# First hats from PSUM, nine sums over thirteen product buffers, and other orders, in a deformable attention followed by a binary convolution

## The chip, the cores and the metric

One core of one Trainium2 chip runs the whole kernel. TensorE (PE) multiplies matrices, VectorE (DVE), ScalarE (ACT) and GpSimd (POOL) work elementwise, SyncE (SP) issues DMAs. The metric is the device time of one execution in microseconds, as the median of several runs. All engines work off their own lists in order; semaphores tie them together.

## The reference

The input x is 4 images of 64 channels and 32 by 32 pixels. Two layers follow each other.

The first is a deformable attention with 8 heads of 8 channels and 4 points for each head:

```
v    = q @ W_value + b_value
off  = q @ W_off + b_off            # an (x, y) offset for each pixel, head and point
attn = softmax over the 4 points of (q @ W_attn + b_attn)
loc  = the pixel's own place + off / 32
out  = sum over points of attn * bilinear(v, loc)
x    = out @ W_out + b_out + q
```

The bilinear sample takes four neighbours of each place, with weights that are products of a hat in y and a hat in x, max(0, 1 - distance).

The second is a 3 by 3 convolution of the signs of x (with a bias ahead) with the signs of its weights times their mean magnitude, a batch norm over all images, the residual, and a PReLU with biases.

## The kernel before

**Layout.** Images are taken in two pairs (g = 0, 1), each with 2 x 64 channels on the 128 partitions. The 1024 pixels are two halves of 512 (yh = 0 the upper, 1 the lower).

**Taps instead of gathers.** Offsets are small, so that every sampled neighbour lies among 16 shifts around a pixel: 4 rows (ZERO, OUTER, MINUS, PLUS) by 4 columns (ZERO, MINUS, PLUS, OUTER). OUTER stands for shifts that only occur in a zone of 12 pixels at the borders, and so it is smaller. A half has 16 taps, the kernel 32 (t = 0 to 31, 0 to 15 the upper half). A tap has 512 columns; with OUTER in one direction 384, in both 288. A case in which an offset is larger than that has a general branch that isn't taken here.

**Steps of one tap.** (1) The hats: ACT computes a distance `Abs(u + shift)` into `tab` (L688) and a hat `Relu(1 - tab)` (L695), where `u` is the position, the offset in PSUM with its bias (L680). (2) DVE multiplies the turned probabilities with a hat in y: `attend(n)`, one for each row of taps (L941). (3) POOL multiplies this with a hat in x into `ap`, `weight(t)` (L864); taps 0 and 1 are DVE's own (L951, `DVE_COLUMNS`). `ap` has `RAP` = 6 buffers. (4) PE spreads the 32 weights of heads and points over the 128 channels, `spread(t)` (L508, from tap 8 on L513), into one of two, later three, PSUM buffers. From tap 8 on the taps go in pairs, and the second tap of each pair (9, 11, ..., 31) is "swapped": it uses the other half of PE and reads values from `vswap`, so both taps of a pair run at the same time. (5) DVE multiplies with the shifted values, `product(t)` (L970), into one of `PR` = 12 buffers `prod`. (6) PE projects the product with W_out and accumulates in PSUM, `project(unit)` (L530).

**Sums.** The projection is linear, so two products of the same output rows can be added first and projected once. `SUM_FROM = {1: 2, ...}` says that product 2 is added into product 1, by an accumulating DMA that POOL issues (L871) behind the weight that `SUMS_BEHIND` names. The sum is one unit, so the six sums leave 26 units of 32. A buffer of `prod` is free for product t + PR when its unit is projected or, for the second summand, when the sum has landed (`product`, L960 to L965).

**Orders.** PE's list is written out by hand: the units in `TAPS_AFTER[t]` are projected behind spread t, the rest (`TAPS_AT_END`) after the last spread, with the first row of the convolution ahead of the very last unit. Between a swapped and an unswapped unit PE waits for the one before. Spread t also waits for product t - 2 (later t - 3), and for its weight. DVE's list is the products in order, with the `attend`s behind those that `ROW_AFTER` names.

**The start.** Logits, offsets (`ps_off`) and values of the upper half come first; the softmax is made in three parts (two quarters of the upper half, then the lower half whole); `turn(yh)` transposes the probabilities into PSUM (L493). ACT's order is: two exponentials, two positions, then distances and hats. Lower values, offsets and logits follow among the first spreads.

## Time and profile before

| | us |
|---|---|
| median of 3 runs | 86.0 (85.94 to 86.25) |
| the profiled execution | 85.9 |
| its span, first to last instruction | 84.1 |
| PE busy | 66.5 |
| DVE busy | 58.7 |
| POOL busy | 47.7 |
| ACT busy | 46.2 |

A row of a timeline has the start, the duration, the engine, the line of the kernel and the operation; x8 says that eight records are merged, and the brackets name the idle time ahead and what ended it. A projection or a spread of one tap is eight matmul records on PE, the weights of one tap one record on POOL, and the products of one tap one record on DVE. No row carries the number of its tap; it follows from the order and the sizes. The chain of waits is followed back from the last instruction, at each step to what released it.

### The profile page before, as it was taken

How to read it: one execution, taken by the hardware profiler on the slowest of the kernel's cores; microseconds unless marked ns; L12 is line 12 of the kernel's file. 1: busy time of each engine (PE TensorE's matmuls, PEld its weight loads, DVE VectorE, ACT ScalarE, POOL GpSimd, SP SyncE). 2: the span in 40 equal slices, each digit the busy share in tenths (PEclk: the TensorE clock that was granted, in tenths of full speed). 3: DMA queues.
4: the chain of work that ended last, by engine and by line, in shares of the span. 5: the costliest groups of instructions: out<-in, count | busy, mean ns of one | idle time of the engine just before them, and what ended most of it. 6: DMA issues, size and time to landing. Idle time of an engine off the chain costs nothing.

```text
span 84.1 us, 1712 instructions
## 1 busy us (share of the span) xinstructions
PE 66.5 (79%) x642; PEld 25.4 (30%) x642; DVE 58.7 (70%) x85; ACT 46.2 (55%) x92; POOL 47.7 (57%) x47
## 2 busy tenths in 40 slices
PE   5999997999799999999999959999799985200000
PEld 4766275223142322132323314222223542200000
DVE  2307978999989999596997889203970067689920
ACT  2401999995599999997000399900000397059500
POOL 7970000879999999999999999950000000009000
PEclk9999999999999999999999999999999999995555
DMA  0917865920599980091006638390000000000195
GB/s 9 295 42 253 250 232 123 224 74 0 97 207 213 213 146 1 0 216 37 0 8 134 119 53 134 64 189 4 0 0 0 8 0 0 0 4 0 24 281 194
DMA packets 3897, 8.09 MB, mean 96 GB/s; under 512 B 560, under 2 KB 1584, under 8 KB 3888
## 3 DMA queue, kind: packets, MB, share of 16 engines
q1 hardware_dynamic: 2320, 4.40, 19.1%
q0 software_dynamic: 1120, 2.88, 19.0%
q10 hardware_dynamic: 448, 0.69, 2.6%
q8 instruction: 5, 0.08, 0.4%
q14 instruction: 4, 0.03, 0.1%
HBM read 2.27 MB, written 1.05 MB: 39 GB/s over the span
## 4 chain that ended last, share of the span: by engine, by line
PE 50%; DVE 19%; POOL 10%; issue 8%; DMA 5%; ACT 2%; DVEq 1%; ACTq 0%; POOLq 0%
PE banks L530 21%; PE banks L513 12%; POOL ap L864 10%; DVE prod L970 6%; DMA win<-w_in_dram 5%; PE banks L562 4%; PE banks L476 3%; PE banks L508 3%; DVE prod L1104 3%; PE banks L459 2%; DVE prod L1115 2%; DVE bns L1075 2%; ACT sg L783 2%; DVE ays L941 1%; PE banks L466 1%
## 5 line engine op out<-in xcount | busy, mean ns | idle before, releaser
L864 POOL TENSOR_TENSOR ap<-ays,hat 128x512 f32<-128x512 f32 (+2 forms) x30 | 36.1, 1592 | 9.7 <-ACT hat L695 9.2
L970 DVE TENSOR_TENSOR prod<-banks,vpad 128x1024 f32<-128x1024 f32 (+2 forms) x20 | 22.1, 1114 | 8.2 <-PE banks L530 5.1
L530 PE MATMUL banks<-prod,wo 64*64 64x512 f32 (+2 forms) x208 | 23.1, 547 | 0.7 <-PE banks L530 0.5
L513 PE MATMUL banks<-ap,cst 32*64 32x512 f32 (+2 forms) x192 | 16.9, 567 | 1.5 <-POOL ap L864 1.0
L888 POOL TENSOR_SCALAR prod<-prod,prm,st 128x512 f32<-128x512 f32 x3 | 2.3, 763 | 19.8 <-ACT st L831 19.8
L970 DVE TENSOR_TENSOR prod<-banks,vswap 128x1024 f32<-128x1024 f32 (+3 forms) x13 | 12.6, 975 | 0.0
L530 PEld LDWEIGHTS banks<-prod,wo 64*64 64x64 f32 x208 | 6.9, 132 | 15.1 <-issue 11.1
L513 PEld LDWEIGHTS banks<-ap,cst 32*64 32x64 f32 x192 | 4.3, 130 | 13.7 <-POOL ap L864 8.1
L688 ACT ACTIVATE tab<-u,cst 128x512 f32<-128x512 f32 x12 | 8.3, 716 | 0.1
L871 POOL DMA_DIRECT2D prod<-prod x6 | 7.3, 1217 | 0.2 <-ACT hat L695 0.2
L695 ACT ACTIVATE hat<-tab 128x512 f32<-128x512 f32 x12 | 7.2, 621 | 0.0
L805 ACT ACTIVATE flag<-banks 1x6 f32<-1x6 f32 x1 | 0.2, 165 | 10.5 <-PE banks L521 10.5
L508 PE MATMUL banks<-ap,cst 64*64 64x384 f32 (+2 forms) x48 | 5.1, 506 | 0.6 <-DVE prod L970 0.6
L941 DVE TENSOR_TENSOR ays<-banks,hat 128x512 f32<-128x512 f32 (+1 forms) x8 | 5.0, 650 | 0.6 <-PE banks L493 0.6
L775 ACT ACTIVATE x1n<-banks,prm 128x512 f32<-128x512 f32 x1 | 0.7, 688 | 8.2 <-PE banks L530 8.2
L562 PE MATMUL banks<-sg,wcb 64*64 64x512 bf16 (+2 forms) x84 | 4.6, 351 | 0.2 <-ACT sg L783 0.2
L724 ACT ACTIVATE ex<-lsub 128x256 f32<-128x256 f32 (+1 forms) x3 | 1.4, 483 | 5.1 <-DVE lsub L903 5.1
L476 PEld LDWEIGHTS banks<-win,xs 128*128 128x128 f32 x32 | 3.9, 191 | 1.1 <-DMA win<-w_in_dram 0.6
L476 PE MATMUL banks<-win,xs 128*128 128x64 f32 x32 | 4.0, 273 | 0.1
L459 PE MATMUL banks<-xs,win 128*64 128x512 f32 x16 | 4.1, 611 | 0.0
L580 PE MATMUL banks<-ones 128*128 128x256 f32 x6 | 2.9, 661 | 1.0 <-POOL ones L851 1.0
L718 ACT ACTIVATE lsub<-lsub,cst 128x384 f32<-128x384 f32 (+1 forms) x6 | 3.5, 580 | 0.2
(84 smaller groups left out, 79.3 us busy)
## 6 DMA issues: line engine op xcount, KB each, us to landing
prod<-prod POOLq DMA_DIRECT2D x4, 512.0 KB, 5.4
vswap<-vpad SPq DMA_DIRECT2D x4, 432.0 KB, 5.5
xs<-x_dram SPq DMA_DIRECT2D x3, 256.0 KB, 4.2
prod<-prod POOLq DMA_DIRECT2D x2, 384.0 KB, 5.4
out_dram<-prod SPq DMA_DIRECT2D x2, 256.0 KB, 3.2
wcf<-w_conv_dram SPq DMA_DIRECT2D x1, 288.0 KB, 4.2
wab<-w_abs_dram SPq DMA_DIRECT2D x1, 288.0 KB, 4.2
xs<-x_dram ACTq DMA_DIRECT2D x1, 256.0 KB, 2.9
```

The lines of the kernel that those rows point to most:

```text
L459: mm = pe.matmul(ps_off[yh][d][g * C:(g + 1) * C, :], wp[:, d, :], chunk(xs, g, yh), start=False, stop=True, skip_group_check=True)
L476: mm = pe.matmul(ps_log[part][:, at:at + C], xs[:, g, q:q + P], wp[:, 2, :], start=False, stop=((n + 1) * P == end and g == G - 1), skip_g ...
L508: mm = pe.matmul(spread_into(t)[rows_out, g, 0:size_of(t)], sel_of(g)[rows_in, rows_out], weights_at(t)[rows_in], start=True, stop=True)
L513: mm = pe.matmul(spread_into(t)[quadrant(i, g, t in SWAPPED)[1], g, 0:size_of(t)], sel_of(g)[rows_in, quadrant(i, g)[1]], weights_at(t)[ro ...
L530: mm = pe.matmul(into, wo[rows_in, rows_in], source, start=False, stop=last, skip_group_check=True)
L562: mm = pe.matmul(ps_y[yh][g][rows_out, first_row * W:last_row * W], wcb[rows_in, ky * K + kx, :], sg[rows_in, g, y0:y0 + last_row - first_ ...
L688: nc.scalar.activation(tab[:, n % 4], u[:, d, yh, :], ACT.Abs, bias=cst[:, c_tap + k:c_tap + k + 1]).then_inc(s_abs, 1)
L695: nc.scalar.activation(hat[:, yh, d, k, :], tab[:, m % 4], ACT.Relu, bias=1.0, scale=-1.0).then_inc(s_hat, 1)
L864: pool.tensor_tensor(into, factor, near, ALU.mult).then_inc(s_ap, 1)
L871: pool.dma_start(prod[:, into % PR, :, 0:size_of(into)], prod[:, more % PR, :, 0:size_of(more)], accum_op=ALU.add).then_inc(s_s2[k % len(s ...
L941: nc.vector.tensor_tensor(ays[:, n % RY, at], ps_att[yh][:, at], hat[:, yh, 1, ky, at], ALU.mult).then_inc(s_ay, 1)
L970: nc.vector.tensor_tensor(as_window(t, prod[:, t % PR, g, 0:n]), as_window(t, spread_into(t)[:, g, 0:n]), v_window(t, g), ALU.mult).then_i ...
```

## The change

What each part does:
- `FROM_PSUM`: the first three distances (y ZERO, x ZERO, x MINUS of the upper half) read the offsets in PSUM directly, with the offset's bias, or that bias plus one (`bias_minus`, a new 128x1 operation). The positions of the upper half are computed behind the first three hats and no longer ahead.
- Tap 1's weight goes from DVE to POOL (`DVE_COLUMNS`, `RA` 3 to 1). The softmax scale of the lower half goes from POOL to DVE.
- PE turns the upper probabilities before it computes the upper values, which go to other banks. Spread 0 comes ahead of the second half of the lower logits. The second turn stands behind spread 4 and no longer behind spread 5.
- DVE stores the upper values behind weight 0; product 0 waits for them. The maximum of the lower logits stands behind product 0. The `attend`s have other places.
- `PR` goes from 12 to 13. Nine sums in place of six, with 23 units in place of 26, and other orders of the units.

```diff
-SUM_FROM = {1: 2, 5: 6, 8: 10, 16: 18, 20: 22, 24: 26}
-SUMS_BEHIND = {6: 1, 9: 5, 15: 8, 23: 16, 26: 20, 29: 24}
-DVE_COLUMNS = [2] + [0] * (ROWS - 1)
+SUM_FROM = {0: 1, 8: 2, 12: 10, 5: 4, 13: 9, 18: 16, 26: 24, 25: 17, 20: 22}
+SUMS_BEHIND = {7: 0, 11: 5, 13: 8, 18: 12, 19: 13, 24: 18, 26: 20, 28: 25, 30: 26}
+DVE_COLUMNS = [1] + [0] * (ROWS - 1)
+FROM_PSUM = [(0, 1, ZERO), (0, 0, ZERO), (0, 0, MINUS)]
...
-        RA, RAP = 3, 6
+        RA, RAP = 1, 6
-        PR = 12
+        PR = 13
-        ps_v = [[bank[0], bank[1]], [bank[5], bank[4]]]
+        ps_v = [[bank[2], bank[3]], [bank[5], bank[4]]]
...
-        TAPS_AFTER = {7: [4], 9: [0, 3], 11: [9, 1], 13: [7], 15: [5, 12], 17: [15], 19: [14, 8], 21: [11], 23: [13],
-                      27: [19, 23, 17], 29: [25, 27, 21, 16], 31: [29]}
-        TAPS_AT_END = [24, 28, 30, 20, 31]
+        TAPS_AFTER = {9: [0, 6, 3], 11: [5, 7], 13: [11], 15: [8], 17: [14], 19: [15], 21: [12], 23: [13], 27: [21, 19, 23],
+                      29: [18, 20, 28], 31: [29, 25, 27]}
+        TAPS_AT_END = [30, 26, 31]
...
-            values(0)
             pe.wait_ge(s_sub, 2)
             logits_bias(2)
+            pe.wait_ge(s_cst, 16)
+            turn(0)
+            values(0)
             pe.wait_ge(s_x[1], 32)
             logits(2, range(NCH // 2))
-            pe.wait_ge(s_cst, 16)
-            turn(0)
-            logits(2, range(NCH // 2, NCH))
-            pe.wait_ge(s_u, 2)
-            base_positions(1, 1)
             for taps in SPREADS:
+                if taps[0] == 1:
+                    logits(2, range(NCH // 2, NCH))
+                    pe.wait_ge(s_vp, G)
                 for t in taps:
                     spread(t)
                 if t == 1:
+                    pe.wait_ge(s_u, 2)
+                    base_positions(1, 1)
                     offsets(1, 1)
...
-                if t == 5:
+                if t == 4:
                     turn(1)
...
             def distances(n):
                 yh, d, k = DISTANCES[n]
+                if (yh, d, k) in FROM_PSUM:
+                    act.wait_ge(s_off, POSITIONS.index((yh, d)) + 1)
+                    if k == MINUS:
+                        act.wait_ge(s_bias, 1)
+                    bias = prm[:, p_off + d:p_off + d + 1] if k == ZERO else bias_minus[:]
+                    nc.scalar.activation(tab[:, n % 4], ps_off[yh][d][:], ACT.Abs, bias=bias).then_inc(s_abs, 1)
+                    return
...
-                pool.wait_ge(s_p, products_done(more, G - 1))
+                pool.wait_ge(s_p, products_done(max(into, more), G - 1))
...
-                if t == 6:
-                    pool.wait_ge(s_rec, 3)
-                    pool.tensor_tensor(grouped(prob[:, 1, :]), grouped(ex[:, 1, :]), spread_points(lrec[:, 1, :]),
-                                       ALU.mult).then_inc(s_prob, 1)
...
-            store_upper_values()
             attend(0)
             weight(0)
-            weight(1)
-            softmax_max(2)
-            ROW_AFTER = [0, 3, 6, 7, 9, 9, 9]
+            store_upper_values()
+            ROW_AFTER = [0, 1, 4, 7, 8, 9, 9]
             for t in range(NT * YH):
                 product(t)
                 if t == 0:
+                    softmax_max(2)
+                if t == 1:
                     softmax_sub(2)
                 if t == 2:
                     softmax_sum(2)
                     softmax_recip(2)
+                    softmax_scale(2)
```

How it moves instructions. ACT, from the first exponentials to the hat PLUS in x (tab is a distance, hat a hat, u a position); before:

```order
L724 ACTIVATE ex<-lsub 128x256 [waits sub_ready] x2
L680 ACTIVATE u<-banks,prm 128x512 [waits offsets_ready,params_in]
L680 ACTIVATE u<-banks,prm 128x512 [waits offsets_ready]
L688 ACTIVATE tab<-u,cst 128x512 [waits positions_ready,const_in]
L688 ACTIVATE tab<-u,cst 128x512 [waits positions_ready]
L695 ACTIVATE hat<-tab 128x512 [waits abs_ready]
L688 ACTIVATE tab<-u,cst 128x512 [waits positions_ready]
L695 ACTIVATE hat<-tab 128x512 [waits abs_ready] x2
L688 ACTIVATE tab<-u,cst 128x512 [waits positions_ready]
L695 ACTIVATE hat<-tab 128x512 [waits abs_ready]
```

and now:

```order
L736 ACTIVATE ex<-lsub 128x256 [waits sub_ready] x2
L694 ACTIVATE tab<-banks,prm 128x512 [waits offsets_ready] x2
L707 ACTIVATE hat<-tab 128x512 [waits abs_ready] x2
L694 ACTIVATE tab<-banks,bias_minus 128x512 [waits shifted_bias_ready,offsets_ready]
L707 ACTIVATE hat<-tab 128x512 [waits abs_ready]
L685 ACTIVATE u<-banks,prm 128x512 [waits offsets_ready] x2
L700 ACTIVATE tab<-u,cst 128x512 [waits positions_ready,const_in]
L707 ACTIVATE hat<-tab 128x512 [waits abs_ready]
```

The two positions moved behind the third hat; up to the fourth hat it is ten operations both times.

POOL, from the weights of taps 16 to 18 on (L864 and L877 are weights, L871 and L884 the issues of sums); before:

```order
L864 TENSOR_TENSOR ap<-ays,hat 128x512 [waits spread_ready,hats_ready,ay_ready] x3
L864 TENSOR_TENSOR ap<-ays,hat 128x384 [waits spread_ready,hats_ready,ay_ready] x4
L864 TENSOR_TENSOR ap<-ays,hat 128x288 [waits spread_ready,hats_ready,ay_ready]
L871 DMA prod<-prod 128x1024 [waits products_ready]
L864 TENSOR_TENSOR ap<-ays,hat 128x512 [waits spread_ready,hats_ready,ay_ready] x3
L871 DMA prod<-prod 128x2x384 [waits products_ready]
L864 TENSOR_TENSOR ap<-ays,hat 128x384 [waits spread_ready,hats_ready,ay_ready]
L864 TENSOR_TENSOR ap<-ays,hat 128x512 [waits spread_ready,hats_ready,ay_ready] x2
L871 DMA prod<-prod 128x1024 [waits products_ready]
```

and now:

```order
L877 TENSOR_TENSOR ap<-ays,hat 128x512 [waits spread_ready,hats_ready,ay_ready] x3
L884 DMA prod<-prod 128x1024 [waits products_ready]
L877 TENSOR_TENSOR ap<-ays,hat 128x384 [waits spread_ready,hats_ready,ay_ready]
L884 DMA prod<-prod 128x1024 [waits products_ready]
L877 TENSOR_TENSOR ap<-ays,hat 128x384 [waits spread_ready,hats_ready,ay_ready] x3
L877 TENSOR_TENSOR ap<-ays,hat 128x288 [waits spread_ready,hats_ready,ay_ready]
L877 TENSOR_TENSOR ap<-ays,hat 128x512 [waits spread_ready,hats_ready,ay_ready]
L884 DMA prod<-prod 128x1024 [waits products_ready]
L877 TENSOR_TENSOR ap<-ays,hat 128x512 [waits spread_ready,hats_ready,ay_ready] x2
L884 DMA prod<-prod 128x2x384 [waits products_ready]
L877 TENSOR_TENSOR ap<-ays,hat 128x384 [waits spread_ready,hats_ready,ay_ready]
L877 TENSOR_TENSOR ap<-ays,hat 128x512 [waits spread_ready,hats_ready,ay_ready]
```

The sums into 12 and 13 stand behind weights 18 and 19, that into 18 behind 24, that into 20 behind 26 as before, and the next row is the sum into 25, behind 28.

PE, behind spread 29 (L530 before and L533 now are projections, two rows for each unit, the other line the spreads); before:

```order
L530 MATMUL banks<-prod,wo 64x512 [waits products_ready]
L530 MATMUL banks<-prod,wo 64x512 x3
L530 MATMUL banks<-prod,wo 64x16x2x12 [waits products_ready]
L530 MATMUL banks<-prod,wo 64x16x2x12 x3
L530 MATMUL banks<-prod,wo 64x384 [waits products_ready]
L530 MATMUL banks<-prod,wo 64x384 x3
L530 MATMUL banks<-prod,wo 64x512 [waits units_projected,sums_ready3]
L530 MATMUL banks<-prod,wo 64x512 x3
L513 MATMUL banks<-ap,cst 64x512 [waits products_ready,gpsimd_tap_weights_ready]
L513 MATMUL banks<-ap,cst 64x512 x3
```

and now:

```order
L533 MATMUL banks<-prod,wo 64x512 [waits units_projected,products_ready]
L533 MATMUL banks<-prod,wo 64x512 x3
L533 MATMUL banks<-prod,wo 64x512 [waits sums_ready3]
L533 MATMUL banks<-prod,wo 64x512 x3
L533 MATMUL banks<-prod,wo 64x16x2x12 [waits products_ready]
L533 MATMUL banks<-prod,wo 64x16x2x12 x3
L533 MATMUL banks<-prod,wo 64x512 [waits units_projected,products_ready]
L533 MATMUL banks<-prod,wo 64x512 x3
L533 MATMUL banks<-prod,wo 64x512 [waits sums_ready2]
L533 MATMUL banks<-prod,wo 64x512 x3
```

Before, four units (25, 27, 21, 16) stand between spread 29 and spread 30, the last of them the sum whose buffer product 28 takes. The second piece is the end of the list now, behind spread 31: units 29, 25, 27, 30, 26.

## Rows read from the trace of the kernel before

**Rows 1.** Chain of waits: start, us, what, where it leaves POOL and at its last projection
```profile
48.47 1.86 POOL ap L864
50.33 0.04 issue
50.37 0.88 PE banks L513 x8
...
66.11 0.73 PE banks L530 x8
```

**Rows 2.** Timeline of PE from spread 24 on
```profile
47.44 1.95 PE L513 MATMUL banks<-ap,cst 32*64 32x512 f32 x24
50.37 0.88 PE L513 MATMUL banks<-ap,cst 32*64 32x384 f32 x8 [0.98 <-POOL ap L864]
51.18 2.22 PE L530 MATMUL banks<-prod,wo 64*64 64x384 f32 x24
53.33 1.11 PE L513 MATMUL banks<-ap,cst 32*64 32x512 f32 x16
54.37 2.38 PE L530 MATMUL banks<-prod,wo 64*64 64x512 f32 x24
...
57.95 1.09 PE L513 MATMUL banks<-ap,cst 32*64 32x512 f32 x8
...
60.49 1.09 PE L530 MATMUL banks<-prod,wo 64*64 64x512 f32 x8 [0.17 <-DVE prod L970]
61.75 3.45 PE L530 MATMUL banks<-prod,wo 64*64 64x512 f32 x32 [0.18 <-PE banks L530]
65.14 0.19 PE L521 MATMUL banks<-over,ones 128*1 128x6 f32 x2
```

**Rows 3.** Timeline of POOL: single weights (L864), issues of sums (L871), the softmax scale
```profile
15.04 1.28 POOL L864 TENSOR_TENSOR ap<-ays,hat 128x512 f32<-128x512 f32 x1 [9.18 <-ACT hat L695]
17.82 1.00 POOL L864 TENSOR_TENSOR ap<-ays,hat 128x384 f32<-128x384 f32 x1 [0.55 <-DVE ays L941]
21.68 1.15 POOL L880 TENSOR_TENSOR prob<-ex,lrec 128x512 f32<-128x512 f32 x1
26.20 1.21 POOL L871 DMA_DIRECT2D prod<-prod  x1 [0.16 <-ACT hat L695]
32.89 1.44 POOL L864 TENSOR_TENSOR ap<-ays,hat 128x384 f32<-128x384 f32 x1
33.83 1.35 POOL L871 DMA_DIRECT2D prod<-prod  x1
...
43.39 0.96 POOL L871 DMA_DIRECT2D prod<-prod  x1
...
46.46 1.65 POOL L864 TENSOR_TENSOR ap<-ays,hat 128x512 f32<-128x512 f32 x1
47.69 1.61 POOL L871 DMA_DIRECT2D prod<-prod  x1
48.47 1.85 POOL L864 TENSOR_TENSOR ap<-ays,hat 128x384 f32<-128x384 f32 x1
...
50.66 2.12 POOL L864 TENSOR_TENSOR ap<-ays,hat 128x512 f32<-128x512 f32 x1
```

**Rows 4.** Timeline of ACT: the first of the ten operations and the last
```profile
8.96 0.69 ACT L680 ACTIVATE u<-banks,prm 128x512 f32<-128x512 f32 x1
...
14.25 0.63 ACT L695 ACTIVATE hat<-tab 128x512 f32<-128x512 f32 x1
```

**Rows 5.** Timeline of DVE: the lower maximum, and products 0, 12 and 28
```profile
14.76 0.68 DVE L897 TENSOR_REDUCE lmax<-banks 128x128 f32<-128x512 f32 x1
15.45 1.23 DVE L970 TENSOR_TENSOR prod<-banks,vpad 128x1024 f32<-128x1024 f32 x1
...
34.54 1.23 DVE L970 TENSOR_TENSOR prod<-banks,vpad 128x1024 f32<-128x1024 f32 x1 [0.87 <-PE banks L513]
...
58.08 1.23 DVE L970 TENSOR_TENSOR prod<-banks,vpad 128x1024 f32<-128x1024 f32 x1 [5.05 <-PE banks L530]
```

**Rows 6.** The line of the six sums' DMAs
```profile
DMA to landing us min/median/max: 4.8/5.4/6.7
```

More of the change, by code:

```diff
@@ L166, in deformable_attention_then_binary_conv @@
         st = sb("st", [P, 17])
+        bias_minus = sb("bias_minus", [P, 1])
         spare = prod[:].rearrange("p r g n -> p (r g n)")
@@ L211, in deformable_attention_then_binary_conv @@
         s_abs = sem("abs_ready")
+        s_bias = sem("shifted_bias_ready")
         s_hat = sem("hats_ready")
@@ L724, in exponentials @@
                 nc.scalar.activation(ex[:, yh, first:end], lsub[:, yh, first:end], ACT.Exp).then_inc(s_exp, 1)
+            act.wait_ge(s_prm, 16)
+            nc.scalar.activation(bias_minus[:], prm[:, p_off:p_off + 1], ACT.Identity, bias=1.0).then_inc(s_bias, 1)
             exponentials(0)
             exponentials(1)
-            act.wait_ge(s_prm, 16)
+            distances(0)
+            distances(1)
+            hats(0)
+            hats(1)
+            distances(2)
+            hats(2)
             positions(0, 1)
@@ L731, in _ @@
             act.wait_ge(s_cst, 16)
-            distances(0)
-            distances(1)
-            hats(0)
-            distances(2)
-            hats(1)
-            hats(2)
             distances(3)
@@ L954, in product @@
                 yh, ky, kx = tap_of(t)
+                if t == 0:
+                    dve.wait_ge(s_vp, G)
                 if yh == 0 and ky == PLUS:
```

## The prediction

> **What bounds the kernel now.** I read the chain of waits first, then PE's timeline, POOL's, and those of ACT and DVE at the places that these two point to. Up to 50.33 us the chain runs over POOL's tap weights, and from there to 66.84 over PE, apart from one product of DVE [rows 1]. So two laws hold in turn. Until spread 27 POOL sets the time: its weight of tap 27 ends at 48.47 + 1.85 = 50.32, and PE's spread 27 starts at 50.37, after 0.98 of idle time [rows 2, 3]. From then on PE has a list to work off, and it ends with the projection of tap 31 at 66.11 + 0.73 = 66.84 [rows 1]. Behind that stand the signs, the rest of the convolution, the batch norm and the output; the change touches none of it. I keep these 84.1 - 66.84 = 17.3 us, and ask when the projection of tap 31 ends now.
>
> **POOL, up to spread 27 (the term that is easy to miss).** POOL's records start ahead of its work (that of the issue at 33.83 starts 0.50 before the weight of 32.89 ends), so I count from end to end. What changes:
> - Start. POOL's weight 2 waits for the hat of column PLUS, the tenth operation of ACT after the two exponentials: from 8.96 to 14.88 [rows 4]. The change reorders these ten and leaves their number: two distances, two hats, a distance and a hat now come ahead of the two positions. The distances read PSUM; a position that reads PSUM today takes 0.69, an operation on SBUF about as much (0.63) [rows 4]. So this hat ends at about 14.9 again, and weight 2 starts at 15.1 where it started at 15.04 [rows 3]: +0.04. POOL's extra weight, tap 1, goes into the 9.18 us that POOL idles here [rows 3]: it needs the sixth of those operations, done at some 12.5, and ends at 13.9. Cost nothing; without that gap 1.3. The small operation that makes the shifted bias stands where ACT waits for the logits, and costs nothing either.
> - The idle 0.55 us ahead of weight 4, for DVE's second row product [rows 3], goes: by the count of DVE below that product is done at 16.6, before weight 3 ends (17.3). -0.55.
> - The softmax scale of the lower half leaves POOL: -1.15 [rows 3]. So does the wait for a hat ahead of sum 5: -0.16 [rows 3].
> - Sums. Each is a DMA that POOL issues between two weights. Its price, from the end of the weight before to the end of the issue: 33.83 + 1.35 - (32.89 + 1.44) = 0.85 for a sum of 512 columns, 47.69 + 1.61 - (46.46 + 1.65) = 1.19 for one of 384 [rows 3]. Ahead of weight 27 there were five (into 1, 5, 8, 16, 20) and now seven (into 0, 5, 8, 12, 13, 18, 20). The two more are of 512 columns: +1.70, and I add 0.1 for the restart behind them.
>
> Sum: 50.32 + 0.04 - 0.55 - 1.15 - 0.16 + 1.80 = 50.3. Weight 27 ends where it ended; what POOL gains is spent on the new sums. Between weights 27 and 29 there was no sum and now stands one (into 25): weight 29 ended at 50.66 + 2.12 = 52.78 [rows 3] and now ends 0.85 later, at 53.6. Between 29 and 31 stands one sum as before, so weight 31 is 0.85 later too, at some 56.7 by the same 3.1 us.
>
> **Is anything else later than POOL at spread 27?** DVE's product 0 started at 15.45 [rows 5]. Now the turn and the hat come earlier, and DVE has the first row product and weight 0 done at 12.6, the two value stores (0.7 each, moved behind them) at 14.0, and product 0 starts when spread 0 ends, about 14.25: -1.2. Between product 0 and 12 DVE now also has the maximum that stood ahead of it (0.68, [rows 5]) and the scale from POOL (some 0.65): +1.3. It was free for product 12 at 34.54 - 0.87 = 33.67 [rows 5], and is so at about 33.8. Nothing is won at the front. PE reached spread 24 at 47.44 [rows 2]; from product 12 to there it has 768 columns of projection less (units 8, 14, 15, 12, 13 behind spread 14, for 5, 12, 15, 14, 8, 11, 13), 1.3 us by the price below. So PE is there at 45.6, or at 46.6 if DVE is an us late, and waits for POOL. Product 24, which spread 27 needs, ends by 48.9 even then. That is the cover of 1.4 to 2 us under which every delay of DVE and ACT ahead of it costs nothing; were it gone, each us would be one of the end.
>
> **PE from spread 27 on.** The price of a run of projections: 1920 columns (24, 28, 30, 20) from 61.75 to 65.14 are 3.39; 1184 columns (19, 23, 17) from 51.18 to 53.33 are 2.15 [rows 2]. The two give 1.685 us per 1000 columns and 0.155 for the switch. A pair of spreads takes 1.04 (53.33 to 54.37). A change from swapped to unswapped units waits some 0.25 (60.49 to 61.75 is 1.26 where one unit and a switch are 1.02) [rows 2]. In the new order:
> - spread 27 from 50.3, 0.81 [rows 2]: 51.1
> - units 21, 19, 23, 1056 columns, 1.94: 53.05
> - spreads 28 and 29: 29 waits for its weight (53.6) and takes its 1.04: 54.7, where the pair alone would end at 54.1
> - units 18, 20, 28, 1408 columns, 2.53: 57.2
> - spreads 30 and 31, whose weights are there: 58.25. Today they take from 57.95 to 60.49, 2.54 [rows 2], as spread 31 stands behind product 28, and that behind 5.05 of DVE idle for the slot of unit 16 [rows 5]. With thirteen slots product 28 follows spread 28 (slot of 15, projected long ago) and ends by 55.9. This is the largest gain: 1.5
> - units 29, 25, 27, 1408 columns, 2.53: 60.8; the change 0.25; units 30, 26, 1024 columns, 1.88: 62.9
> - flag, first row of the convolution and unit 31, from 65.14 to 66.84, 1.70 [rows 1, 2]: 64.6
>
> That is 2.2 earlier than 66.84: 512 columns (0.86), the stall (1.5), one change of two (0.25), one switch (0.15) and 0.07 at the start, less the wait for weight 29 (0.6). The profiled execution was 85.9, its span of 84.1 and 1.8 around it, so 83.7. The median of the runs shown is 86.0; the same step from there is 83.8. I give **83.7**.
>
> **Landing of sums.** Sums take 4.8 to 6.7 from issue to landing [rows 6]. Sum 13 is issued at about 39 and lands at 44.4, or 46 if it shares the engines with sum 12, issued 1.9 ahead; PE and product 22 (now its slot) ask at 44.5. The wait for POOL behind them covers 1.5. Sum 25 is issued at 51.6 and there by 58.3 at the worst, when product 30 asks; sum 26 at 55 and by 61.7, and PE asks at 61.9. All at no cost, if narrowly. The Trainium skill (DMA: Bandwidth & Descriptors, Anatomy of one DMA — SWDGE (gpsimd) path) has a fit of 2.0 us and the bytes at 436 GB/s, which makes an estimate of 3.2 us for 512 KB; the trace has a median of 5.4, and the measurement decides. By the page's figure none of these would be narrow, and the sum would be the same.
>
> **The rivals.**
> A, POOL does not bind. If its long records hide waits that go too, PE does spreads 24 to 31 as it comes to them from 45.6: spread 27 at about 48.0, no wait for weight 29, the same list: 61.7, **81**. For it: PE would be ready. Against it: nothing in POOL's rows shows a wait there [rows 3]. A milder form: an issue costs 0.5 less, as its record overlaps the weight; then the end is some 0.7 earlier, 83.0.
> B, the issues cost more: the 1.19 of the sum of 384 for each of the three new ones, and the front half a us late: 3 x 0.35 + 0.5 = 1.5 later, **85.2**.
> C, slower. The closest sums stood 4.30 apart (43.39 and 47.69 [rows 3]); now 12 and 13 stand 1.9 apart. If POOL holds the second issue until the first has landed, it stands 5.4 - 1.9 = 3.5 us, weight 27 ends at 53.8, and the time is **87.2**. It is a loss from a stall of 2.2 us on. Nothing in the trace shows two of them in flight. The Trainium skill (SBUF — State Buffer, SBUF: two separate sides, the note on the "DVE blocks DMA" trap) names another way to a stalled issue: GpSimd can't write descriptors while DVE runs a two-port copy. Issues here took 0.96 to 1.61 beside DVE's products [rows 3], and the added ones stand beside the same.
> D, no effect: C's stall of about 2 us, or the reordered operations of ACT wait for each other and weight 2 starts 2 us later: 85.9.
>
> **How the numbers follow.** Forecast (82.8 to 84.6) 0.62; A with its milder form (80.5 to 82.8) 0.15; B (84.6 to 85.5) 0.12; D 0.05; C 0.06. The range for 8 in 10 takes in the near parts of A and B: 82.3 to 85.2. About 0.5% is what a measurement of this kernel can tell from no change. Faster by over that 0.87, within it 0.07, slower 0.06.
>
> **What would show it.** Right: POOL without a gap from 15.1 to 56.7, weight 27 ending at 50.3; PE idle for POOL ahead of spreads 25 to 27; spreads 30 and 31 in about 1.05; DVE's idle 5.05 broken up; unit 31 ending near 64.6. Wrong: weight 2 later than 15.5, issues of sums over 1.3 each, a second issue that waits for a landing, or PE waiting for DVE where I have POOL.

## The result: 88.7 us, slower where faster was forecast

The changed kernel takes 88.66 us (88.47 to 89.45, 4 runs) against 86.12 for the kernel before on the same chip: a ratio of 1.029, interval 1.021 to 1.038. The forecast was 83.7, with 85.2 as the upper end. The profiled execution took 88.74, with a span of 86.9. Medians here and below are of all runs of a kernel; the ratios and their intervals leave out those that were disturbed.

A first reading, in the order of the prediction. The chain of waits (start, us, what) at the front, and at its last projection:

```profile
22.88 4.45 DVE prob L931
27.38 1.11 PE banks L496 x4
28.49 2.67 PE banks L511 x16
...
68.69 0.73 PE banks L533 x8
```

Before, the chain ran over PE here (it reaches POOL's weights only at 39.66); now it stands for 4.45 us on one instruction of DVE. That is the softmax scale of the lower half, 128x512, which the change moved from POOL to DVE. The groups of instructions (busy us, mean ns | idle before, releaser) show it in one mean that its two small forms hide, and in PE's wait:

```profile
L931 DVE TENSOR_TENSOR prob<-ex,lrec 128x256 f32<-128x256 f32 (+1 forms) x3 | 5.1, 1739 | 0.0
L496 PE MATMUL banks<-cst,prob 128*128 128x128 f32 x8 | 1.8, 362 | 4.1 <-DVE prob L931 4.1
```

POOL's timeline, to be read beside [rows 3], around that instruction and at the sums 12 and 13 that rival C was about:

```profile
22.05 0.97 POOL L884 DMA_DIRECT2D prod<-prod  x1
22.82 3.94 POOL L877 TENSOR_TENSOR ap<-ays,hat 128x512 f32<-128x512 f32 x3
30.18 1.02 POOL L877 TENSOR_TENSOR ap<-ays,hat 128x384 f32<-128x384 f32 x1 [3.42 <-PE banks L511]
...
41.46 1.26 POOL L884 DMA_DIRECT2D prod<-prod  x1
...
43.02 1.56 POOL L884 DMA_DIRECT2D prod<-prod  x1
```

PE's timeline, to be read beside [rows 2], at the front and from spread 24 on:

```profile
27.38 1.11 PE L496 MATMUL banks<-cst,prob 128*128 128x128 f32 x4 [3.95 <-DVE prob L931]
28.42 3.45 PE L511 MATMUL banks<-ap,cst 64*64 64x384 f32 x24
...
55.12 0.87 PE L516 MATMUL banks<-ap,cst 32*64 32x384 f32 x8 [1.12 <-POOL ap L877]
55.92 2.00 PE L533 MATMUL banks<-prod,wo 64*64 64x384 f32 x24
57.86 1.74 PE L516 MATMUL banks<-ap,cst 32*64 32x512 f32 x16
...
62.05 1.09 PE L516 MATMUL banks<-ap,cst 32*64 32x512 f32 x16
```

From spread 27 to the end of unit 31 it is 68.69 + 0.73 - 55.12 = 14.3 us, the 14.3 of the prediction. All of the miss lies ahead of spread 27: it stands at 55.12, where 50.3 was forecast.

**The clock.** Behind PE's 3.95 us of idle time the granted clock falls. PE takes 3.45 us over three spreads there. The windows (us, busy us of PE, PEld, DVE, ACT, POOL, then the clock, the DMA share and GB/s):

```profile
23.00:27.00 4.00, 0.43 (x4) 0.00 (x0) 4.00 (x1) 3.44 (x7) 3.76 (x4) 1.00 0.91 180
27.00:28.00 1.00, 0.62 (x3) 0.62 (x4) 1.00 (x2) 1.00 (x3) 0.00 (x0) 0.71 0.98 194
28.00:31.00 3.00, 3.00 (x19) 0.87 (x17) 2.60 (x4) 3.00 (x7) 0.82 (x1) 0.53 0.65 165
31.00:32.00 1.00, 0.82 (x12) 0.24 (x8) 0.82 (x2) 1.00 (x2) 0.89 (x2) 1.00 0.03 8
```

PE ran near the 1.2 GHz level for some three us after it had stood, and came back to 2.4. Against the kernel of experiment 2, which has no such stall, PE reaches spread 8 at 32.29 instead of 26.99, 5.3 later. Of that 0.8 is an earlier difference at the start (the bias matmuls ahead of the first logits took 1.95 us here and 1.25 to 2.04 in the other runs, changed or not), 3.75 the longer wait for the scale, and 0.75 is left, which is not the whole price of the clock. From the second turn up to spread 8 PE's matmuls take 4.5 us here and 3.1 in experiment 2, 1.4 more; but experiment 2 stands for 1.0 us between them (for products of DVE and for a weight of POOL), and this kernel only for 0.4.

**Why the instruction stands.** DVE's scale ends at 27.32. POOL's three weights (8, 9, 10) end at 22.82 + 3.94 = 26.76, and POOL then has nothing to do: weight 11 needs the factor buffer of a spread that itself waits for the scale (3.42 of idle). So the scale ended 0.56 after POOL ran dry. Both of its inputs, ex and lrec, are in SBUF, as are both of POOL's. From the first product on, every other operation that DVE has beside POOL's weights, in either kernel, reads at most one tile from SBUF (products, row products and lsub read a bank as well) and takes its usual time. The Trainium skill states the rule (SBUF — State Buffer, SBUF: two separate sides): a DVE operation "with two SBUF inputs (only against a GpSimd op that reads SBUF)" and a GpSimd operation exclude each other, whichever starts first, "for the whole instruction". The trace agrees that they exclude each other. It goes beyond the page on how long: DVE did not get in between weights 8, 9 and 10, but stood until POOL had run out of them.

### The profile page after: what moved, and what is told of

Read it like the earlier page. It is cut to its first block, busy times and chain, and to the rows that moved or that the text cites. A ratio compares the mean times of both kernels' runs of the same rounds, so it can differ in the third digit from the quotient of the medians.

```text
span 86.9 us, 1670 instructions
## 1 busy us (share of the span) xinstructions
PE 66.7 (77%) x618; PEld 26.1 (30%) x618; DVE 62.7 (72%) x85; ACT 46.7 (54%) x93; POOL 50.7 (58%) x50
## 4 chain that ended last, share of the span: by engine, by line
PE 42%; DVE 27%; POOL 16%; issue 7%; ACT 2%; DVEq 1%; POOLq 0%
PE banks L533 14%; POOL ap L877 13%; PE banks L516 7%; DVE prob L931 5%; DVE prod L981 5%; PE banks L511 4%; PE banks L565 4%; PE banks L583 3%; POOL prod L884 3%; DVE prod L1116 3%; PE banks L479 2%; DVE lrec L925 2%; DVE prod L1127 2%; PE banks L496 2%; PE banks L469 2%
## 5 line engine op out<-in xcount | busy, mean ns | idle before, releaser
L877 POOL TENSOR_TENSOR ap<-ays,hat 128x512 f32<-128x512 f32 (+2 forms) x31 | 40.5, 1653 | 12.5 <-ACT hat L707 9.1
L533 PE MATMUL banks<-prod,wo 64*64 64x512 f32 (+2 forms) x184 | 19.8, 539 | 0.2 <-PE banks L533 0.2
L884 POOL DMA_DIRECT2D prod<-prod x9 | 12.4, 1378 | 0.1
L533 PEld LDWEIGHTS banks<-prod,wo 64*64 64x64 f32 x184 | 5.9, 132 | 13.3 <-issue 9.9
L511 PE MATMUL banks<-ap,cst 64*64 64x384 f32 (+2 forms) x56 | 7.1, 612 | 0.0
L700 ACT ACTIVATE tab<-u,cst 128x512 f32<-128x512 f32 x9 | 6.2, 715 | 0.2
L931 DVE TENSOR_TENSOR prob<-ex,lrec 128x256 f32<-128x256 f32 (+1 forms) x3 | 5.1, 1739 | 0.0
L496 PE MATMUL banks<-cst,prob 128*128 128x128 f32 x8 | 1.8, 362 | 4.1 <-DVE prob L931 4.1
L906 DVE TENSOR_REDUCE lmax<-banks 128x64 f32<-128x256 f32 (+1 forms) x3 | 1.5, 510 | 3.8 <-PE banks L479 3.8
```

What stands on the lines that cost most here:

```text
L511: mm = pe.matmul(spread_into(t)[rows_out, g, 0:size_of(t)], sel_of(g)[rows_in, rows_out], weights_at(t)[rows_in], start=True, stop=True)
L533: mm = pe.matmul(into, wo[rows_in, rows_in], source, start=False, stop=last, skip_group_check=True)
L700: nc.scalar.activation(tab[:, n % 4], u[:, d, yh, :], ACT.Abs, bias=cst[:, c_tap + k:c_tap + k + 1]).then_inc(s_abs, 1)
L877: pool.tensor_tensor(into, factor, near, ALU.mult).then_inc(s_ap, 1)
L884: pool.dma_start(prod[:, into % PR, :, 0:size_of(into)], prod[:, more % PR, :, 0:size_of(more)], accum_op=ALU.add).then_inc(s_s2[k % len(s ...
L931: nc.vector.tensor_tensor(grouped(prob[:, yh, first:end]), grouped(ex[:, yh, first:end]), spread_points(lrec[:, yh, first // POINTS:end // ...
```

## Experiments

Theory T1: the scale on DVE is the whole of the miss, and it stands because it and POOL's weights both read SBUF alone. Rival T2: the new front (other bank roles, other orders) or the sums lose it elsewhere, and the scale only shows a wait that would stand somewhere else. Times below are medians, with the kernel before on the same chip behind them; "from the first maximum to the signs" is a stretch of the trace that leaves out the scatter of the start.

**1. The scale back on POOL**, all else as changed.

```diff
+                if t == 7:
+                    pool.wait_ge(s_rec, 3)
+                    pool.tensor_tensor(grouped(prob[:, 1, :]), grouped(ex[:, 1, :]), spread_points(lrec[:, 1, :]),
+                                       ALU.mult).then_inc(s_prob, 1)
...
-                    softmax_scale(2)
```

> The changed kernel, with only the lower softmax scale given back to POOL, behind the issue of sum 0. Theory 1 (the loss comes from DVE's scale, both of whose inputs lie in SBUF, and which stands as long as POOL works through its row of weights): DVE has no operation over 1.3 us in the first half, PE's idle 3.95 ahead of the second turn shrinks under 1 us, its clock does not fall, and the sum of the prediction holds with POOL's 1.15 us added: 84.9, up to 85.8 if the 0.95 us by which the changed kernel was late before its first logits belongs to it. Theory 2 (the stall has another cause, such as nine sums crowding DMA or the new orders; the scale only stands where it shows): within 0.5 us of the changed kernel, 88.2 to 88.9.

84.94 us against 86.68, ratio 0.984 (0.974 to 0.994). POOL pays 1.23 us for the scale and PE waits 0.80 for it, not 3.95; spread 27 is at 51.42. T1 holds in direction and size.

**2. The scale on DVE, its reciprocals in PSUM.** The same instruction at the same place beside the same weights, but one of its inputs is in a bank that is free then.

```diff
-                nc.vector.reciprocal(lrec[:, yh, at], lsum[:, yh, at]).then_inc(s_rec, 1)
+                into = bank[7][:, at] if yh else lrec[:, yh, at]
+                nc.vector.reciprocal(into, lsum[:, yh, at]).then_inc(s_rec, 1)
...
+                at = slice(first // POINTS, end // POINTS)
...
-                                        spread_points(lrec[:, yh, first // POINTS:end // POINTS]), ALU.mult).then_inc(s_prob, 1)
+                                        spread_points(bank[7][:, at] if yh else lrec[:, yh, at]), ALU.mult).then_inc(s_prob, 1)
```

> The changed kernel; the scale stays on DVE in the same place, but the reciprocals of the lower half (128 columns) are written to and read from PSUM, into the bank whose logits have been read, so that the scale has one input in SBUF and one in PSUM. Theory 1 (two SBUF inputs against POOL's weights): the scale takes 0.6 to 0.8 in place of 4.44 beside the same weights of POOL, and the time is that of the prediction, 83.7, up to 84.7 with the late start. Theory 2a (the operation is slow by its form, a broadcast over four points of 512 columns): it stays at 4.4 and the time at 88.6.

83.88 us against 86.68, ratio 0.967 (0.958 to 0.977); three of its four runs lie at 83.69 to 84.02, the fourth at 88.96. The timelines of DVE and POOL at the scale:

```profile
21.10 0.96 DVE L926 RECIPROCAL banks<-lsum 128x128 f32<-128x128 f32 x1
22.10 0.69 DVE L933 TENSOR_TENSOR prob<-ex,banks 128x512 f32<-128x512 f32 x1
...
22.03 4.94 POOL L877 TENSOR_TENSOR ap<-ays,hat 128x512 f32<-128x512 f32 x4
```

0.69 instead of 4.44, beside four weights without a gap. This is the sharpest of the runs, since it changes neither the order, nor the engine, nor the size of anything. The result is also close to the kernel that the prediction described. The rest of PE's timeline:

```profile
50.75 0.88 PE L516 MATMUL banks<-ap,cst 32*64 32x384 f32 x8 [1.12 <-POOL ap L877]
...
53.49 1.73 PE L516 MATMUL banks<-ap,cst 32*64 32x512 f32 x16
...
57.67 1.09 PE L516 MATMUL banks<-ap,cst 32*64 32x512 f32 x16
```

**3. The kernel before with only this part of the change**: the scale moved to DVE.

```diff
-                if t == 6:
-                    pool.wait_ge(s_rec, 3)
-                    pool.tensor_tensor(grouped(prob[:, 1, :]), grouped(ex[:, 1, :]), spread_points(lrec[:, 1, :]),
-                                       ALU.mult).then_inc(s_prob, 1)
...
                     softmax_recip(2)
+                    softmax_scale(2)
```

> The kernel before, with one part of the change alone: the lower softmax scale moves from POOL to DVE, behind the reciprocal. Theory 1: it starts near 21.6 and waits for POOL's weights 7, 8 and 9 to end (about 25.0), so it takes about 4 us; behind it POOL stands until product 6, and the whole is 3 to 3.5 us slower than before, 89.0 to 89.5. Theory 2: DVE has 0.65 more and POOL 1.15 less, 85.0 to 86.7.

88.63 us against 86.68, ratio 1.024 (1.014 to 1.034): this part alone brings the loss. But the scale took 1.47 us, where some 4 were expected. The timelines of DVE, POOL and PE:

```profile
21.85 1.47 DVE L918 TENSOR_TENSOR prob<-ex,lrec 128x512 f32<-128x512 f32 x1
...
21.69 1.07 POOL L864 TENSOR_TENSOR ap<-ays,hat 128x288 f32<-128x288 f32 x1
24.86 2.51 POOL L864 TENSOR_TENSOR ap<-ays,hat 128x512 f32<-128x512 f32 x2 [2.10 <-DVE ays L937]
28.53 1.21 POOL L871 DMA_DIRECT2D prod<-prod  x1 [1.16 <-DVE prod L966]
...
24.33 0.88 PE L508 MATMUL banks<-ap,cst 64*64 64x384 f32 x8 [2.18 <-DVE prod L966]
```

Here POOL had one weight to do and then waited for a row product that stands behind the scale on DVE. So the scale stood 0.8 us only, and the rest of the loss is POOL's: 2.10 + 1.16 of idle time for work of DVE that the scale had pushed back. PE, which had stood for 2.18 us up to 24.33, ran at a granted clock of 0.50 from 26 to 28. The direction was right; the size (1.95 us slower, where 3 to 3.5 was expected) and my account of it were not.

**4. The changed kernel with five factor buffers (RAP) instead of six**, one run. If the scale stands until POOL runs dry, POOL runs dry one weight sooner.

```diff
-        RA, RAP = 1, 6
+        RA, RAP = 1, 5
```

> The changed kernel with five buffers of POOL's weights in place of six. Theory 1: POOL runs out of work one weight of 512 columns (1.24 us) earlier, since weight 10 and no longer weight 11 waits for spread 5; the scale ends then, and takes 3.2 in place of 4.44. The time falls by 0 to 1.2 us, less what fewer buffers cost later. If POOL's row of weights is not what it waits for: 4.4 again.

The time was 87.8, in a single run. The timelines of DVE and POOL at the scale:

```profile
21.95 3.25 DVE L931 TENSOR_TENSOR prob<-ex,lrec 128x512 f32<-128x512 f32 x1
...
21.88 2.76 POOL L877 TENSOR_TENSOR ap<-ays,hat 128x512 f32<-128x512 f32 x2
```

The scale took 3.25 us (3.2 expected). Put together:

| kernel | weights in a row beside the scale | their end | scale's end | scale took |
|---|---|---|---|---|
| changed | 3 | 26.76 | 27.32 | 4.44 |
| 4, five buffers | 2 | 24.64 | 25.20 | 3.25 |
| 3, before + scale on DVE | 1 | 22.76 | 23.32 | 1.47 |
| 2, reciprocals in PSUM | 4 | 26.97 | 22.79 | 0.69 |

In the first three the scale ends 0.56 after the last weight, however many there were. T1 stands, and T2 falls for the front.

**5. Only the nine sums, thirteen product buffers and the unit orders**, on the kernel before (front and scale as before). The places of the sums and the lists of units are those of the change; for room, DVE's weights have two buffers and no longer three.

```diff
-SUM_FROM = {1: 2, 5: 6, 8: 10, 16: 18, 20: 22, 24: 26}
+SUM_FROM = {0: 1, 8: 2, 12: 10, 5: 4, 13: 9, 18: 16, 26: 24, 25: 17, 20: 22}
...
-        PR = 12
+        PR = 13
```

> The kernel before, with the other half of the change alone: thirteen product buffers, nine sums, the new places of the sums and the new order of the units; the start, the scale on POOL and the weights stay (the buffers of DVE's weights go from 3 to 2 for room; DVE has two weights). By the sum of the prediction: weight 27 ends at 50.32 + 1.8 = 52.1, since none of POOL's gains at the front is there to pay for the sums, and from spread 27 the list takes 14.3, so unit 31 ends at 66.4 and the time is 85.5. If the nine sums themselves cost more than their issues (landings late, engines of DMA crowded), 86.5 or more.

The 85.5 is missed, and the other branch (86.5 or more, with late landings) came: 88.99 us against 86.65, ratio 1.032 (1.021 to 1.044). PE's timeline, and the windows (columns as above):

```profile
32.45 3.94 PE L530 MATMUL banks<-prod,wo 64*64 64x512 f32 x24 [4.10 <-DMA prod<-prod]
...
28.00:30.00 2.00, 0.35 (x4) 0.00 (x0) 2.00 (x3) 2.00 (x5) 2.00 (x4) 1.00 1.03 219
30.00:32.00 2.00, 0.00 (x0) 0.00 (x0) 1.64 (x3) 2.00 (x4) 2.00 (x3) 1.00 1.01 208
32.00:34.00 2.00, 1.55 (x8) 0.60 (x12) 0.00 (x0) 1.94 (x6) 2.00 (x4) 0.56 0.86 147
```

PE waits 4.10 us for sum 0 to land. POOL issues it at 23.43, behind its scale, and it lands some 8.9 us later (the issue, and the landings of all nine sums):

```profile
23.43 1.00 POOL L871 DMA_DIRECT2D prod<-prod  x1
...
DMA to landing us min/median/max: 4.4/5.1/8.9
```

In experiment 2 it is issued at 21.26 and PE does not wait for it. What makes it slow is argued only: the transfers of the lower swapped values are issued at 23.32, just ahead of it (at 24.07 in experiment 2, well behind it), and the DMA engines are full until 32 (share 1.01 to 1.03). But they are nearly as full in experiment 2 (0.95 to 1.06 from 24 to 30), so what is left of the argument is the order of issue, and no run changed that alone. The price is shown: with these lists of units, which ask for sum 0 early, the old front costs PE 4.10 us at sum 0.

**6 to 8. Where the added sums stand**, all on the kernel of experiment 2: sum 25 behind weight 29 (6); three sums later and unit 20 behind unit 30 (7); no sum 20, its units 20 and 22 projected apart, and sum 25 behind weight 29 (8).

```diff
-SUMS_BEHIND = {7: 0, 11: 5, 13: 8, 18: 12, 19: 13, 24: 18, 26: 20, 28: 25, 30: 26}
+SUMS_BEHIND = {7: 0, 11: 5, 13: 8, 18: 12, 19: 13, 24: 18, 26: 20, 29: 25, 30: 26}   # 6
+SUMS_BEHIND = {7: 0, 11: 5, 13: 8, 18: 12, 19: 13, 24: 18, 28: 20, 29: 25, 31: 26}   # 7
+SUMS_BEHIND = {7: 0, 11: 5, 13: 8, 18: 12, 19: 13, 24: 18, 29: 25, 30: 26}           # 8
```

The lines marked 6, 7 and 8 are the three versions; 7 also moves unit 20, and 8 takes `20: 22` out of `SUM_FROM` and projects unit 22 behind unit 20.

> The version with reciprocals in PSUM (83.9), with the issue of sum 25 behind weight 29 and no longer behind weight 28. Weight 29 ends 0.85 earlier, and the pair of spreads 28 and 29 takes 1.04 in place of 1.66. If PE alone sets the end from spread 27 on, the time falls by 0.6, to 83.3. If weight 31 (its end does not move) or the later landing of sum 25 takes over, by 0 to 0.3.

> The same version with sum 20 behind weight 28, sum 25 behind 29, sum 26 behind 31, and unit 20 projected behind unit 30. Weight 27 ends 1.2 earlier (49.5), and weight 31 0.85 earlier, at 56.3. POOL, which then sets the start of spreads 30 and 31 in place of 27: 56.4 against 57.67, and with a list behind it that is 0.6 longer: the time falls by 0.6 to 0.7, to 83.2. If the issues of sums were not on POOL's path: no change.

> The same version without sum 20 (products 20 and 22 are projected apart), sum 25 behind weight 29. POOL has 1.19 less ahead of weight 27, PE has 384 columns (0.65) more behind it. Where POOL sets the start of spread 27 and PE the rest, weight 27 ends at 49.5 and the list is 14.3 - 0.6 + 0.65: the time falls by 1.1 against 83.9, to 82.8. If PE is the bound all the way, it rises by 0.65.

**10 and 11. Experiments 8 and 2 again, side by side** (6 runs each), since the starts scatter by more than the differences.

> The version without sum 20 once more, in five rounds, beside e11 on the same chip, since its three undisturbed executions lay between 82.76 and 84.24. From its first logits to the last signs it took 1.1 us less than the version with nine sums; if the rest is the scatter of the start and of the tail, 1.0 to 1.2 less than e11 in the median, about 83.

> The version with the reciprocals in PSUM and all else as changed, once more in five rounds: 83.9 as measured, 2.5 to 2.8 under the kernel before of the same chip.

| kernel | time, us | before there | ratio (interval) | first maximum to signs, us |
|---|---|---|---|---|
| before | 86.12 | | | 66.87 - 6.71 = 60.2 |
| changed | 88.66 | 86.12 | 1.029 (1.021 to 1.038) | 69.45 - 7.66 = 61.8 |
| 2, reciprocals in PSUM | 83.88 | 86.68 | 0.967 (0.958 to 0.977) | 65.07 - 6.87 = 58.2 |
| 11, the same again | 84.77 | 86.35 | 0.982 (0.976 to 0.987) | 65.89 - 7.67 = 58.2 |
| 6, sum 25 later | 84.49 | 86.65 | 0.980 (0.969 to 0.990) | 64.42 - 6.84 = 57.6 |
| 7, three sums later | 84.25 | 86.65 | 0.977 (0.965 to 0.990) | 64.71 - 7.42 = 57.3 |
| 8, no sum 20 | 84.14 | 86.65 | 0.975 (0.962 to 0.989) | 63.61 - 6.55 = 57.1 |
| 10, the same again | 83.82 | 86.35 | 0.966 (0.958 to 0.975) | 64.31 - 7.21 = 57.1 |

In the stretch the trace shows what was expected: 0.6 for sum 25, since spreads 28 and 29 need not wait for weight 29 any more (1.11 in 6, where 2 has 1.73), 0.9 for the three later sums (0.6 to 0.7 expected), and 1.1 for leaving out sum 20 as well. The whole times were missed: 84.49, 84.25 and 84.14, where 83.3, 83.2 and 82.8 had been worked out from the 83.88 of experiment 2. That kernel itself took 84.77 in experiment 11, 1.6 under the kernel before and not 2.5 to 2.8. Of the whole time 6 and 7 can't be told from 2. Only 10 against 11, on one chip, shows it there too: 0.95 us, with intervals that don't overlap. Experiment 8's kernel is the best of all, 2.5 to 3.4% under the kernel before.

**9. Only the front**: experiment 2's front, with the six sums, orders and twelve buffers of the kernel before.

```diff
-SUM_FROM = {0: 1, 8: 2, 12: 10, 5: 4, 13: 9, 18: 16, 26: 24, 25: 17, 20: 22}
-SUMS_BEHIND = {7: 0, 11: 5, 13: 8, 18: 12, 19: 13, 24: 18, 26: 20, 28: 25, 30: 26}
+SUM_FROM = {1: 2, 5: 6, 8: 10, 16: 18, 20: 22, 24: 26}
+SUMS_BEHIND = {6: 1, 9: 5, 15: 8, 23: 16, 26: 20, 29: 24}
```

> The new front with the reciprocals in PSUM, and behind it the six sums, twelve product buffers and orders of the kernel before. If each half counts for itself: weight 27 ends at 50.32 + 0.04 - 0.55 - 1.15 - 0.16 = 48.5; PE could be at spread 24 at about 46.9 (47.44 less the 0.5 that its waits for POOL shrink), spread 27 starts at 48.9 in place of 50.37, and the old list of 16.5 follows: 1.5 faster than before, 84.4. If DVE or PE are the bound there once POOL is early: 85.0 to 86.

A miss again: 87.48 us against 86.35, ratio 1.015 (1.007 to 1.022). POOL, free of the scale, ended weight 9 at 24.7 instead of 26.0, and then stood 2.04 us ahead of sum 5, which takes in product 6, and that one waits for its spread on PE:

```profile
21.16 3.55 POOL L877 TENSOR_TENSOR ap<-ays,hat 128x288 f32<-128x288 f32 x3
26.75 1.21 POOL L884 DMA_DIRECT2D prod<-prod  x1 [2.04 <-PE banks L511]
```

**12. The same with sum 5 behind weight 11**, to see whether this wait is what eats the gain.

```diff
-SUMS_BEHIND = {6: 1, 9: 5, 15: 8, 23: 16, 26: 20, 29: 24}
+SUMS_BEHIND = {6: 1, 11: 5, 15: 8, 23: 16, 26: 20, 29: 24}
```

> The front alone (maximum rules, reciprocals in PSUM, the scale on DVE, the kernel before's six sums, unit orders and twelve product buffers), with one change: sum 5 is issued behind weight 11 rather than behind weight 9. With sum 5 behind weight 9, POOL had ended weight 9 at 24.7 us and stood 2.04 us for product 6 before it could issue (26.75, against 26.20 in the kernel before), and the kernel ran in 87.48 us where 84.4 had been expected. Theory: that wait ate the gain of POOL's lighter front. With two weights between, product 6 (done by 27.2) lets the issue through with no wait, POOL has 2.0 us less idle time, less what the six factor buffers then make it wait; weight 27's spread stands at 49.3 to 50.0 in the place of 51.24, and with the list of 16.4 us behind it the last signs come 1.2 to 1.9 us earlier: 85.6 to 86.3 us. Rival: the list of the kernel before is bound elsewhere (its six sums, or PE's own order ahead of spread 27), so the time stays at 87.3 to 87.6 us and the idle time moves to another row of POOL.

The rival of that expectation won: 87.72 us against 86.82, ratio 1.008 (1.003 to 1.013). The wait of 2.04 is gone, and two others are there, ahead of sums 8 and 16:

```profile
27.41 1.31 POOL L884 DMA_DIRECT2D prod<-prod  x1
28.20 5.26 POOL L877 TENSOR_TENSOR ap<-ays,hat 128x512 f32<-128x512 f32 x4
34.28 0.90 POOL L884 DMA_DIRECT2D prod<-prod  x1 [0.82 <-DVE prod L983]
34.89 8.62 POOL L877 TENSOR_TENSOR ap<-ays,hat 128x512 f32<-128x512 f32 x8
45.00 0.87 POOL L884 DMA_DIRECT2D prod<-prod  x1 [1.49 <-DVE prod L983]
```

What hardly moves is PE. From its first projection to spread 27, in the kernel before, in 9 and in 12:

```profile
25.37 0.85 PE L530 MATMUL banks<-prod,wo 64*64 64x384 f32 x8
...
26.23 0.85 PE L533 MATMUL banks<-prod,wo 64*64 64x384 f32 x8
...
51.24 0.88 PE L516 MATMUL banks<-ap,cst 32*64 32x384 f32 x8 [0.91 <-POOL ap L877]
...
26.89 0.85 PE L533 MATMUL banks<-prod,wo 64*64 64x384 f32 x8
...
51.88 0.87 PE L516 MATMUL banks<-ap,cst 32*64 32x384 f32 x8 [0.89 <-POOL ap L877]
```

It is 25.00 ([rows 2] has spread 27 at 50.37), 25.01 and 24.99 us. With six sums PE has hardly a gap in this stretch (in the kernel before it is busy for 23.66 of the 23.90 us from 25.40 to 49.30), so its list sets when product 18 is done. POOL reaches sum 16 without a wait in the kernel before and waits for that product in 9 (0.31) and 12 (1.49), and then has the weights up to 27 to do. POOL's relief ran into that wait in both places of sum 5; another order of the units was not tried. The new front only puts PE's first projection later: 19.8 us behind the first maximum in 9 and 12, 18.7 before. Of these 1.1 us, 0.9 are two waits of PE for products of DVE, 0.30 and 0.59 behind the second turn, in both runs; the kernel before has none there. That they come from DVE's added scale (0.69) is likely but not shown.

## Why the prediction was wrong, point by point

- **The failed step: "the scale from POOL (some 0.65)"**. It stands in the paragraph that asks whether anything is later than POOL. The scale took 4.44 us. 0.65 was the time of an operation of that size on DVE with POOL idle. In the kernel before, each operation of DVE with two SBUF inputs (the upper scale, weights 0 and 1 at 13.55 to 14.84) ran ahead of POOL's first weight at 15.04 [rows 3], so no row could price one beside POOL. The prediction gave a single price where it needed a bound from both sides, since its rows don't show such an operation in that place. It cited the page of the Trainium skill that has the rule (SBUF — State Buffer, SBUF: two separate sides), but for a stall of issues, which did not come.
- **The cover** of "1.4 to 2 us under which every delay of DVE and ACT ahead of it costs nothing". The delay was 3.75, so it would not have been enough. But it was the wrong measure too: POOL has six factor buffers, and gets them back from PE's spreads. A stall of PE that is longer than POOL's lead reaches POOL itself, here as 3.42 us of idle time, and POOL is the bound. Against experiment 2, PE is 4.5 us late at spread 8 and still 3.6 at spread 27 (55.12 against 50.75, less 0.8 of the start). That a stall of PE also costs clock was in no case of the prediction.
- **POOL's sum held** once the scale is out of the way. Weight 27 ends at 50.70 in experiment 2 (50.3 forecast). Of the 0.4, 0.33 is there from the start: weight 2 starts at 15.43 where 15.1 was forecast, and 0.16 of that is a first maximum that was later than before. The issues cost what they did before (in the changed kernel 0.83 to 0.91 from end to end for the sums of 512 columns, 1.33 and 1.18 for the two of 384, into 5 and 20), though their records reach 1.84; so **rival B** and the milder form of A fell. None waits for another's landing (43.02 follows 41.46), so **rival C fell**. Spread 27 waits 1.12 us for POOL, so **rival A** itself fell as well, and so did **rival D**, as weight 2 is not 2 us late.
- **PE's list held**: 14.3 us in the changed kernel and in experiment 2, 14.3 forecast. Spreads 30 and 31 take 1.09 together; the 5.05 us of DVE's idle time [rows 5] are gone, and 1.83 are the most ahead of one product there:

```profile
59.09 1.22 DVE L981 TENSOR_TENSOR prod<-banks,vpad 128x1024 f32<-128x1024 f32 x1 [1.56 <-PE banks L516]
...
63.27 1.22 DVE L981 TENSOR_TENSOR prod<-banks,vpad 128x1024 f32<-128x1024 f32 x1 [1.83 <-PE banks L516]
```

- **The forecast of 83.7** is thus the time of experiment 2's kernel (83.88 and 84.77; 2.8 and 1.6 under the kernel before, where 2.2 was the sum). It is right for a kernel that differs from the changed one in where 128 columns of reciprocals are kept.
- **"Until spread 27 POOL sets the time"** was read too widely. The chain of the kernel before does not run over POOL's weights up to 50.33, but only from 39.66 on; from 12.83 to there it runs over DVE and PE. The page of that kernel has the shares of its whole chain by engine:

```profile
PE 50%; DVE 19%; POOL 10%; issue 8%; DMA 5%; ACT 2%; DVEq 1%; ACTq 0%; POOLq 0%
```

With the nine sums, which take projections out of PE's list, POOL's sum gave the time all the same, as the point above shows. With six, POOL and PE are both full, and experiments 9 and 12 show that POOL's relief alone buys nothing. The prediction spent that relief on the new sums and so did not need this, but the expectation of 84.4 for experiment 9 did.
- **The landings** were at no cost in the changed kernel (4.4 to 6.1 us), as forecast "if narrowly". But that kernel runs late. In experiment 2 they take 4.8 to 7.6 us, over the 6.7 that the prediction took as the worst, and its chain of waits does run over one, of sum 5:

```profile
26.69 5.58 DMA prod<-prod
32.31 1.36 PE banks L533 x16
```

PE was free for this unit at 32.22, so it cost 0.1 us; in experiment 1 it cost 0.53. Experiment 5 shows how far it can go: 8.9 us for one of them.

## What to carry to other kernels

Before an operation moves to another engine, look at where its operands are kept, and at what its new neighbours read: here an instruction of DVE with both inputs in SBUF waited as long as POOL had such work in a row, and one operand in PSUM freed it. A duration from a row holds for its surroundings; if the trace has the operation only while the neighbour idles, its price beside a busy one is unknown and needs bounds, here up to the length of POOL's queue. And of parts that are made together (less work on POOL, fewer projections on PE) try each alone: here one alone loses about 1%, the other 3%, and both together, with the scale's operand moved, gain 2 to 3%.

## What the runs showed of the hardware

- With both inputs in SBUF, DVE did not get its turn between two of POOL's operations. It stood over three (3.9 us), two (2.7) and the rest of one (0.9), and each time ended 0.56 us after the last.
- With the reciprocals in PSUM the same operation took 0.69 us beside the same weights, although it still reads one tile from SBUF and writes there.
- After 3.95 us without a matmul PE's granted clock read 0.71 and 0.53 for four us, and three spreads took 3.45 us, where they took 2.45 in experiment 2 at 1.00. In experiment 5 it read 0.56 behind 4.10 us of idle time, in experiment 3 0.50 from 26 to 28, where PE had stood for 2.18 us up to 24.33.
- The sums, of 384 and 512 KB from SBUF into SBUF, landed in 4.4 to 6.1 us in the changed kernel and in 4.8 to 7.6 in experiment 2. In experiment 5 one took 8.9, which was issued 0.1 us behind transfers of the swapped values (DMA share 1.01 to 1.03).
